# A two-layer tower: embedding and first projection as one pipeline, the key-major triangle zeroed by GpSimd, and loads moved between queues

## The reference

```python
h = E1[ids] @ W2.T + b2 + pos_emb                     # rank 32 -> 256
h = h + attn0(layernorm(h))       # 16 heads of 16, rotary positions, causal softmax, W_O
h = h + ffn0(layernorm(h))        # shared squared-relu expert; routed experts with truncated weights
h = h + attn1(layernorm(h))       # 16 heads, causal windows 256 ... 4, values = keys, gates, Wproj
h = h + ffn1(layernorm(h))        # 8 SwiGLU experts, top 2, and a shared one
# attn0, per head:
Q, K, V = (x @ W.T for W in (W_Q, W_K, W_V));  Q, K = rope(Q), rope(K)
out = softmax(where(causal, Q @ K.T / 4, -inf)) @ V
```

## Time and profile before

| what | us |
|---|---|
| median of 3 runs | 1930.79 |
| lowest and highest | 1738.61, 1936.46 |
| the profiled execution: device time | 1737.24 |
| its span | 1735.5 |
| PE busy | 1332.6 (77%) |
| DVE busy | 873.5 (50%) |
| ACT busy | 669.5 (39%) |
| POOL busy | 639.0 (37%) |

### The profile page before, as it was taken

One profiled execution on the slowest core, in us unless ns is written; L12 is line 12 of the kernel. 1 busy time (PEld: TensorE's weight loads), 2 busy tenths in 40 slices (PEclk: granted clock), 3 DMA queues, 4 the chain that ended last, 5 costly groups with the idle time before them and its releaser, 6 DMA issues. The chain is left out here.

```text
span 1735.5 us, 31930 instructions
## 1 busy us (share of the span) xinstructions
PE 1332.6 (77%) x10933; PEld 1041.6 (60%) x10934; DVE 873.5 (50%) x1815; ACT 669.5 (39%) x1256; POOL 639.0 (37%) x587
## 2 busy tenths in 40 slices
PE   2699499999997876555189866631897899999997
PEld 1377255555555765544167555521896688888886
DVE  3677667667772783667455355420343233333332
ACT  1377045555554553232045443310342233333332
POOL 7244455555403220256910000077000345444453
PEclk8799589999998996666599988765898899999999
DMA  1044777777620002335344231000002643454331
GB/s 47 4 162 178 219 223 240 240 234 230 205 53 14 1 1 87 117 115 152 88 99 110 48 111 49 13 13 1 24 30 70 222 120 54 120 160 120 82 55 23
DMA packets 122924, 179.46 MB, mean 103 GB/s; under 512 B 26068, under 2 KB 83868, under 8 KB 122820
## 3 DMA queue, kind: packets, MB, share of 16 engines
q1 hardware_dynamic: 94260, 117.18, 22.2%
q0 software_dynamic: 28560, 60.91, 13.6%
HBM read 104.76 MB, written 74.31 MB: 103 GB/s over the span
## 5 line engine op out<-in xcount | busy, mean ns | idle before, releaser
L1440 DVE TENSOR_REDUCE att_top<-att_psS 128x4 f32<-128x512 f32 (+2 forms) x192 | 196.0, 1037 | 82.4 <-PE att_psS L1327 82.3
L1411 ACT ACTIVATE att_prob<-att_psS 128x1024 f32<-128x1024 f32 (+1 forms) x192 | 169.2, 883 | 174.9 <-PE att_psS L1347 174.4
L2597 POOL DMA_INDIRECT out<-ffn1c_y,ffn1c_table x72 | 114.5, 1590 | 179.3 <-DMA out<-ffn1c_y,ffn1c_table 96.8
L2586 POOL DMA_INDIRECT ffn1c_rows<-normed_rows,ffn1c_table x72 | 70.7, 982 | 152.6 <-DVE ffn1c_gate L2758 128.8
L1321 PE MATMUL att_psS<-att_ka,att_qa 48*128 48x384 f32 (+3 forms) x512 | 107.5, 430 | 24.2 <-DMA att_ka<-k_parts 19.7
L2738 DVE TENSOR_TENSOR ffn1c_hid<-ffn1c_psG,ffn1c_sil 128x512 f32<-128x512 f32 x72 | 49.8, 692 | 145.6 <-PE ffn1c_psG L2638 145.6
L1341 PE MATMUL att_psS<-att_qa,att_ka 50*128 50x256 f32 (+3 forms) x512 | 99.6, 401 | 13.8 <-DVE att_top L1440 13.8
L2638 PE MATMUL ffn1c_psG<-ffn1c_w_h,ffn1c_xh 128*128 x288 | 97.3, 419 | 12.6 <-DMA ffn1c_w_l<-experts_lo 6.0
L1321 PEld LDWEIGHTS att_psS<-att_ka,att_qa 48*128 48x128 f32 x512 | 51.9, 199 | 88.9 <-issue 43.2
L1376 PE MATMUL att_psO<-att_prob,values 128*32 128x512 f32 (+3 forms) x1024 | 99.8, 464 | 0.0
L2417 PE MATMUL ffn1b_psG<-ffn1s_xh,ffn1s_w_h 128*128 (+1 forms) x256 | 55.6, 301 | 50.1 <-issue 44.7
(11 more groups left out here) (385 smaller groups left out, 3593.8 us busy)
## 6 DMA issues: line engine op xcount, KB each, us to landing
prep_raw<-in_w_all POOLq DMA_DIRECT2D x27, 512.0 KB, 4.6
experts_hi<-prep_hi POOLq DMA_DIRECT2D x27, 512.0 KB, 3.8
experts_lo<-prep_lo POOLq DMA_DIRECT2D x27, 512.0 KB, 6.1
ffn1c_w_h<-experts_hi SPq DMA_DIRECT2D x8, 1536.0 KB
ffn1c_w_l<-experts_lo SPq DMA_DIRECT2D x8, 1536.0 KB
qkv_near<-near_keys SPq DMA_DIRECT2D x32, 320.0 KB, 4.2
q_parts<-qkv_part SPq DMA_DIRECT2D x8, 1024.0 KB, 4.0
k_parts<-qkv_part SPq DMA_DIRECT2D x16, 512.0 KB, 5.8
```

Of the source, the lines that this page charges most:

```text
L1411: act.activation(dst, src, ACT.Exp, scale=0.25).then_inc(s["exp"], 1)
L1440: dve.tensor_reduce(dst, src, AX.X, ALU.max).then_inc(s["max"], 1)
L2586: pool.indirect_dma_start(out=rows[:, t.buf, :], out_offset=None, in_=dram["rows"], in_offset=bass.IndirectOffsetOnAxis(ap=table[:, t.valu ...
L2597: pool.indirect_dma_start(out=rows_out, in_=y[:, t.buf, :], in_offset=None, out_offset=bass.IndirectOffsetOnAxis(ap=table[:, t.value:t.val ...
```

## The change

- `embed`, `project_rope` and the block of marks become one block, `front`. The tables of positions (with bias) and of the rank-32 embedding are multiplied once by the projection's weights; a tile's row with its values, and its queries with its keys, are then three matmuls of 512 columns each: a matrix of ones-on-the-diagonal times the position table's high and low part, and the turned rank terms times a rank table (`sums`). The mean is taken out of the tables; the inverse deviation is applied as ACT and DVE read PSUM. POOL gathers 20 tiles, then one tile and one rotation by turns.
- `front` also loads units 0 to 2 of the attention (`pairs.sp_scores_in`). SP no longer waits for the stores; ACT does, in `exps` of unit 1, whose probabilities lie where `part` was. The rows of -1 of the key operand are set by DVE (three units) in `front` and by POOL (three) in the attention.
- In the attention the `sooner` matmuls go. POOL zeroes the upper triangle of the probabilities instead (`triangle`), and `values` waits for it. Values 0 and 1 stand between the last query scores and the last key scores of their round, values 2 and 3 between those of step 2 of the next.
- The pieces' loads and stores are issued by SP; POOL keeps the two arithmetic operations, with the triangles between and behind them.
- The four weights of `out_ffn_sq` are loaded and split during the last rounds (`NextWeights`).
- `project_local`: PE multiplies before it turns the next rows, ACT takes values before the next high parts, DVE multiplies near keys between the second and the third tile's bias, and sums behind the fourth; the last `near_values` is DVE's.

```diff
--- before.py
+++ after.py
...
+class Pairs:
+
+
+    LOADED, EARLY, QROWS = 6, 3, 48
+
...
+    def sp_scores_in(self, sp, u):
...
+        sp.wait_ge(self.s_out[b % 2], 16 * 3 * (b // 2 + 1))
...
+def front(nc, a, res, ident, marks, s_got, pairs, next_weights, va):
...
+    R3 = 3 * RANK
+    FIRST = 20
...
+                if 1 <= b <= pairs.EARLY:
+                    pairs.sp_scores_in(sp, b - 1)
...
+                src = rows[:, TG * g:TG * (g + 1), :]
+                pool.tensor_copy(cat[:, g % 2, :, 0:2, :], src.unsqueeze(2).to_broadcast([P, TG, 2, RANK])).then_inc(s["cath"], 1)
+                pool.wait_ge(s["cath"], g + 1)
+                pool.tensor_tensor(cat[:, g % 2, :, 2, :], src, cat[:, g % 2, :, 0, :].bitcast(F32), ALU.subtract
...
+            for t in range(FIRST):
+                gather(t)
+                if t == FIRST // 2 - 1:
+                    terms(0)
+            pool.wait_ge(s["w"], 64)
+            for m in range(NT):
+                if FIRST + m < NT:
+                    gather(FIRST + m)
+                if m % TG == 0 and m // TG + 1 < B:
+                    terms(m // TG + 1)
+                pool.wait_ge(s["qs"], m + 1)
+                if m >= 2:
+                    pool.wait_ge(s["rot3"], m - 1)
...
+                pool.tensor_tensor(dst, src[:, :, ::-1, :], sn, ALU.mult).then_inc(s["rot2"], 1)
...
+            def sums(ps, m, high, low, table, signal):
+                pe.matmul(ps, one[:], high[:, m % TG, :], start=True, stop=False)
+                pe.matmul(ps, one[:], low[:, m % TG, :], start=False, stop=False)
+                pe.matmul(ps, eS[0:R3, (m // TG) % 2, m % TG, :], table[0:R3, :], start=False, stop=True
+                          ).then_inc(signal, 1)
...
+                if i + 1 < NT:
+                    row_and_values(i + 1)
+                if i < NT:
+                    queries_and_keys(i)
...
+                if i % TG == 1 and i // TG + 1 < B:
+                    turn_ranks(i // TG + 1)
+                if i >= 2:
+                    turn_back(i - 2)
...
+            for at in range(pairs.EARLY):
+                pairs.minus_rows(dve, at)
...
+            for i in range(NT + 3):
+                if i < NT:
+                    row_stats(i)
...
+                if 1 <= i <= NT:
+                    by_cosine(i - 1)
...
+                if i < NT:
+                    invert(i)
...
+                if 2 <= i <= NT + 1:
+                    turned(i - 2)
+                if i >= 3:
+                    low_qk(i - 3)
...
@@ -572,9 +698,9 @@
...
             for b in range(B):
+                products(b)
                 if b + 1 < B:
                     turn_rows(b + 1)
-                products(b)
                 gate_logits(b)
...
@@ -630,9 +756,9 @@
...
             for b in range(B):
+                values(b)
                 if b + 1 < B:
                     high_rows(b + 1)
-                values(b)
                 first_term(b)
...
@@ -677,8 +803,7 @@
...
-            near_values(B - 1)
-            pool.wait_ge(s["pv3"], B)
...
+            def near_values(b):
+                dve.wait_ge(s["sdone"], 3 * b + 3)
+                dve.wait_ge(s["pv3"], b)
+                dve.tensor_tensor(pv[:].rearrange("p n t (h d) -> p (n t h) d", d=DK),
+                                  near[:, b % 3].rearrange("p n t (h d) -> p (n t h) d", d=DK),
+                                  pw[:, b % 2].rearrange("p n t h -> p (n t h)").unsqueeze(2).to_broadcast([P, NW * TG * DH, DK]),
+                                  ALU.mult).then_inc(s["pv1"], 1)
+                dve.wait_ge(s["pv1"], b + 1)
+                dve.tensor_tensor(pv[:, 0:2], pv[:, 0:2], pv[:, 2:4], ALU.add).then_inc(s["pv2"], 1)
+                dve.wait_ge(s["pv2"], b + 1)
+                dve.tensor_tensor(attn[:, tiles_of(b), PW:D], pv[:, 0], pv[:, 1], ALU.add).then_inc(s["pv3"], 1)
+                dve.wait_ge(s["pv3"], b + 1)
...
@@ -764,9 +904,13 @@
             dve.wait_ge(s["edged"], 2)
             for n in range(B + 1):
                 if n < B:
-                    rows(n)
+                    rows(n, (0, 1))
                 if n >= 1:
                     near_products(n - 1)
+                if n < B:
+                    rows(n, (2, 3))
+                if n >= 1:
+                    near_sums(n - 1)
...
+            near_values(B - 1)
...
+            def triangle(v, j):
+                pool.wait_ge(s["exp"], 6 * v + (2, 4, 5, 6)[j])
+                own = prob[v % 2][:, :, START[j]:START[j] + P]
+                pool.affine_select(out=own, in_=own, compare_op=ALU.is_ge, fill=0.0, base=0, pattern=[[0, HG], [1, P]],
+                                   channel_multiplier=-1).then_inc(s["zero"], 1)
+
+            for at in range(pairs.EARLY, LOADED):
+                pairs.minus_rows(pool, at)
+            for u in range(NU + 3):
+                if u < n_pieces:
+                    upper(pool, u)
+                if u >= 3:
+                    triangle(u - 3, 0)
+                if u < n_pieces:
+                    lower(pool, u)
+                if u >= 3:
+                    triangle(u - 3, 1)
+                    triangle(u - 3, 2)
+                if 0 <= u - n_pieces - 3 < len(next_weights.ws):
+                    next_weights.pool_split(pool, u - n_pieces - 3)
+                if u >= 3:
+                    triangle(u - 3, 3)
 
...
-            for u in range(AHEAD):
-                scores_in(u)
+            sp_load(sp, 0)
+            sp_load(sp, 1)
             for u in range(NU + 1):
                 if u >= 1:
                     maxima_out(u - 1)
-                if u + AHEAD < NU:
+                if 1 <= u <= n_pieces:
+                    sp_store(sp, u - 1)
+                if 1 <= u < n_pieces - 1:
+                    sp_load(sp, u + 1)
+                if u == n_pieces + 1:
+                    sp_stored(sp)
+                    next_weights.sp_load(sp)
+                if pairs.EARLY <= u + AHEAD < NU:
                     scores_in(u + AHEAD)
                 if u >= 1:
...
-                    for part in range(2):
-                        for g in range(2):
-                            r = slice(64 * g, 64 * g + 64)
-                            mm = pe.matmul(psS[:, bank, g, col:col + P], half[r, part, :], sooner[r, part, :],
-                                           start=False, stop=True, tile_position=(64 * g, 0), skip_group_check=True)
                 mm.then_inc(s["scoresB"], 1)
...
-                pe.wait_ge(s["exp"], 6 * w + (2, 4, 5, 6)[j])
+                pe.wait_ge(s["zero"], TG * w + j + 1)
...
@@ -1383,14 +1567,16 @@
                 for n in range(6):
                     if u < NU:
                         query_scores(u, n)
+                    if n == 5 and 0 <= u - 3 < NU:
+                        values(u - 3, 0)
+                        values(u - 3, 1)
+                    if n == 2 and 0 <= u - 4 < NU:
+                        values(u - 4, 2)
+                        values(u - 4, 3)
                     if 0 <= u - 3 < NU:
                         key_scores(u - 3, n)
                     if n == 1 and 0 <= u - 1 < NU:
                         turn_top(u - 1)
-                    if n >= 4 and 0 <= u - 3 < NU:
-                        values(u - 3, n - 4)
-                    if n <= 1 and 0 <= u - 4 < NU:
-                        values(u - 4, n + 2)
                     if n == 3 and 0 <= u - 4 < NU:
...
+                if n == 0 and v == 1:
+                    for m in range(2):
+                        act.wait_ge(pairs.s_out[m], 16 * 3 * (B // 2))
...
-
-            @block.sync
-            def _(sp):
-                for w, done in zip(ws, s_raw):
-                    sp.dma_start(w["raw"][:], w["src"]).then_inc(done, 16)
...
-                for n, w in enumerate(ws):
-                    pool.wait_ge(s_raw[n], 16)
-                    pool.tensor_copy(w["hi"][:], w["raw"][:]).then_inc(s["hi"], 1)
-                    pool.wait_ge(s["hi"], n + 1)
-                    pool.tensor_tensor(w["lo"][:], w["raw"][:], w["hi"][:].bitcast(F32), ALU.subtract).then_inc(s["wt"], 1)
...
-                pe.wait_ge(s["wt"], len(ws))
+                pe.wait_ge(next_weights.s_lower, len(ws))
...
+    def sp_load(sp, n):
+        if n >= 2:
+            sp.wait_ge(s_lo, n - 1)
+        sp.dma_start(raw[:, n % 2, :], raw_dram[n]).then_inc(s_raw[n % 2], 16)
+
+    def sp_store(sp, n):
+        par = n % 2
+        sp.wait_ge(s_lo, n + 1)
         for part, dst in ((hi, hi_dram), (lo, lo_dram)):
-            pool.dma_start(dst[n], part[:, par, :].bitcast(F32)).then_inc(s_stored[par], 16)
-        if n + 1 == n_cut:
-            pool.wait_ge(s_stored[0], 32 * (n_cut // 2 + 1))
-            pool.wait_ge(s_stored[1], 32 * (n_cut // 2))
-    return piece, n_cut
+            sp.dma_start(dst[n], part[:, par, :].bitcast(F32)).then_inc(s_stored[par], 16)
...
```

(46 more changed lines are left out.)

594 lines of the change are left out of this document (306 added, 288 removed).

## The result

The changed kernel took 1586.2 us, the median of four runs (1576.4 to 1595.4). It is compared with the two of the four runs of the kernel before that were level with the profiled one (1738.6 and 1740.8 us, the others 1930.8 and 1936.5), and since none of its own four lay 11% up, rival 5 did not come. The ratio is 0.912, with an interval of 0.904 to 0.919: 8.8% faster. Forecast were 1586 us and a range of 1555 to 1775. The sum was right, but three of its terms were not, and their errors had opposite signs.

What follows compares the result with a forecast made beforehand. No engine bounds the whole; stages were priced separately: front -70, attention -28, out_ffn_sq -5, second projection -48, together -151 us against 1737.2, giving 1586 us. The range was 1555 to 1775 with both run levels, 1555 to 1640 for the forecast alone.

Steps and rivals of the forecast that it cites:

- rival 5: Whole kernel: the change works but the time is taken at the upper run level, 1761 us; chance 0.27.
- Front, -70: Start to first score: about 125 us instead of 195.1, at 2.8 us a tile; -76 to -64.
- Attention, -28: Attention without masks: units of 9.7 us in 24 rounds with a piece, saving 28 us; range -4 to -38.
- The ring through POOL: Attention: POOL's triangles, upper and lower with values 0 and 1, keys and exp bound a unit at 9.6 us.
- so it lands near 12: Attention: the next piece's load lands near 12 us of the round, upper wants it at 11; 0 to 1 us.
- rival 1: Attention: POOL's ring is longer, by dearer triangles or a late piece; units 10.3 to 10.7, 1605 us; chance 0.12.
- Rival 2: Front and second projection: PE's clock stays at 1.2 GHz, giving 1637 us; chance 0.08.
- The cold start: First attention rounds: losing DVE's memsets and the cold start saves about 5 us.
- out_ffn_sq, -5: Start of out_ffn_sq: PE's 6.62 us wait for lower halves shrinks to about 2, saving 5 us.
- Second projection, -48: project_local: batches of 14.8 us instead of 21.6 over seven steps, saving 48 us; range -20 to -52.
- The ring broke: Second projection: reordering frees low_rows from the ring with PE's products, leaving DVE's own 14.2 us a batch.
- rival 3: Second projection: DVE's product collides with POOL's sum, adding 2 us a batch, 14 in all, 1600 us; chance 0.08.

Runs made afterwards that it cites:

- experiment 4: Kernel with the early piece load, but only pieces 0 and 1 loaded and split repeatedly, result not the reference's: 1470.6 us in one run.
- experiment 6: Kernel with the early piece load, each triangle zeroed twice by a second affine_select: 1607.2 us in one run.
- experiment 2: Changed kernel, SP issuing the load of piece u+1 ahead of maxima_out and the two stores: 1480.4 us, ratio 0.895.
- experiment 10: Changed kernel with DVE's order in the second projection put back, near product behind all four bias sums: 1520.0 us in one run.
- experiment 1: The changed kernel again, unaltered, on a chip where the kernel before has 1656 us: 1504.9 us, ratio 0.909.
- experiment 3: Changed kernel plus 23 unread 512-column matmuls on PE in the last three steps of front: 1509.1 us, ratio 0.914.
- experiment 5: Kernel with the early piece load, plus SP loading unit 3 as soon as the attention begins: 1553.2 us, ratio 0.893.
- experiment 9: Kernel with early piece load and early unit 3, plus unread matmuls keeping PE busy in front's last steps and rounds 0 to 2: 1481.2 us, ratio 0.893.

## Why the prediction was right

**Front, -70, measured -75.8.** The mechanism is right (POOL and DVE pace it, the store and reload are gone). The term that was mis-sized is the tile: I took 2.8 us with 2.5 as the best case, and it is 2.44. DVE's six operations of a tile take 2.83 us together and overlap by 0.06 to 0.07 each, so the best case was the rule. POOL's 2.9 a tile was too much as well: gathers with other work between them lose the pause of 0.3 us ahead of each, and twelve tiles with a gather passed at about 2.5. The set-up ended later than the 29 us that I had; DVE got into its pace only at 41. That took back a part.

**Attention, -28, measured -13.6.** This is the step that failed, and in three places. (1) The ring through POOL is about 8.0 and not 9.6 (experiments 4 and 6): values 0 run before the second triangle is there. This alone would have given a larger gain, with units at 8.48. The triangle itself was right: 0.63 us where I took 0.62. (2) "so it lands near 12, when upper wants it at about 11. It may cost 0 to 1 us a unit" was the right place, and it was my rival 1 by its cause. The wait is 1.4 us on the average of all pieces and up to 4.9. A piece took 6.9 us to land, where 4.6 was the median before. Its place in the queue has a part in this: issued ahead of the two stores, in experiment 2, it took 5.9, and the second store 6.2 instead of 4.7. How much is due to fuller transfers (a DMA share of 0.76 over the attention, 0.63 before) was not separated. (3) What I left out is what the stall does to the clock: after PE's 1.81 us of waiting shown above, two rounds, mostly at 1.2 GHz, were 3.2 and 4.6 us longer than 8.48. PE's waits for POOL from 170 us on add up to 13.3 us; by my estimate the 50 us at half the clock cost another 25. Rival 2 looked for this in the front and the second projection. In the front the clock was 1.00 from 40 to 115 us, and in the second projection it was 0.77 with DVE as the bound; it came in the attention. With the load earlier the stage takes 304.3 and 301.5 us instead of 330.3 and 337.8. The cold start, where I had hoped for some of 5 us, gave 1.5: the first four intervals took 42.3 us and 43.7 before.

**out_ffn_sq, -5, measured -4.4.** As forecast: the wait of 6.62 us is now 2.09, for DVE's first split. The timeline of the changed kernel:

```profile
457.12 1.94 PE L1712 MATMUL ffn0a_psA<-m_ident,values 128*128 128x128 f32 x8 [1.23 <-PEq L1413]
461.15 1.94 PE L1712 MATMUL ffn0a_psA<-m_ident,values 128*128 128x128 f32 x8 [2.09 <-DVE ffn0a_al L1854]
```

**Second projection, -48, measured -55.5.** The ring broke as described, and DVE's own work is the batch: 14.07 where 14.2 + 0.6 were reckoned, 5 us over seven steps. The collision of rival 3 would have added 2 a batch; it added nothing in most batches, since POOL's sum ends as the product starts. Where they do meet it is real: 4.96 and 4.00 us in experiment 10, against 2.82 and 1.56 apart. The Trainium skill (GPSIMD Engine Reference, Specifications) names that collision for DVE instructions with two SBUF inputs; the trace agrees, with these numbers.

**The rest.** 877.8 against 875.0, as forecast within 3 us.

The sum hit because the attention gave 14 us too little, while front and second projection gave 13 too much. That these cancel is luck: it was not because each step was right.

## What to carry to other kernels

Where two engines and a transfer feed a busy PE, price a stall of PE by the clock that it may cost as well: here a stall of 1.8 us came with two rounds that were 7.8 us longer together, though another of the same length came with none. A load whose buffer has long been free should stand ahead of the stores and the waits in its queue, not behind them. Moving it was worth 24.5 us here, more than the whole attention part of the change. And a gain that equals the forecast is to be compared stage by stage before the reasons are believed.

The best kernels are those of experiments 2, 5 and 9, at 0.893 to 0.895 of the kernel before, against 0.909 to 0.912 for the change as it is.

## What was not expected of the hardware

The shared expert holds a stretch in which PE runs its instructions 2 to 3.5 us apart, with "issue" as the only reason in the trace, while ACT and DVE hardly run at all. It is there in all six traces taken where the kernel before has 1738 us, before and after the change, and not in those of experiments 1 to 3, where it has 1656. PE in the changed kernel, then the 100 us around it, then the same 100 us of experiment 1:

```profile
1047.20 0.37 PE L2605 MATMUL ffn1b_psY<-ffn1s_w_h,ffn1b_act_h 128*128 128x256 f32 x1 [2.42 <-issue]
...
1050.01 0.37 PE L2605 MATMUL ffn1b_psY<-ffn1s_w_h,ffn1b_act_h 128*128 128x256 f32 x1 [2.44 <-issue]
```

```profile
1011.00:1111.00 100.00, 45.06 (x304) 42.95 (x305) 16.73 (x41) 15.96 (x39) 43.48 (x45) 0.67 0.04 11
```

```profile
1001.50:1101.50 100.00, 98.89 (x822) 97.88 (x821) 43.91 (x105) 39.44 (x98) 45.24 (x46) 1.00 0.10 30
```

That is most of the 72 us by which the last stretch of the table is shorter in experiment 1 (805.8), and with it most of what the chips differ by: the last stretch takes 875 to 880 us in those six traces, and 803 to 808 in the seven others. What starves the engines there was not tried.
